# Routed expert blocks with deeper buffers: six row buffers instead of four, three weight buffers instead of two, and each block's rows issued one block earlier

## The chip, the cores and the metric

The kernel is one launch on 1 core of a Trainium2 chip. Its time is device microseconds (us), measured over whole executions; before the change the median of three is 2961.47 us (2958.9 to 2984.51). All durations below come from one further execution, taken with the hardware profiler.

## The reference

A layer stack on 8192 tokens (32 x 256) of width 128, in float32. Attention "a" works over the 256 positions of a sequence, attention "b" over the 32 rows at each position. After each of them comes the same expert layer:

```
x = x + attn_a(layernorm(x));  x = x + ffn(layernorm(x))
x = x + attn_b(layernorm(x));  x = x + ffn(layernorm(x))

_expert(h, g, u, d) = einsum('...i,hi->...h', silu(h @ g.T) * (h @ u.T), d)     # 128 -> 352 -> 128
scores, idx = top_k(softmax(x @ wr.T + rb), 2);  scores = scores / scores.sum()
ffn(x) = _expert(x, shared) + sum over the 2 chosen of 7 experts: score * _expert(x, rg[e], ru[e], rd[e])
```

So each token is computed by one shared expert and by two of seven routed ones.

## The kernel before, in words

There are two halves, A and B, one for each attention. In each half 16 passes of 512 tokens compute attention, the shared expert and the routing. A pass stores its result to DRAM (`x2` in half A, `out` in half B; the profile shows them as `x` and `out_x`) and scatters every token's normalised row twice, once for each chosen expert, into a DRAM buffer `sent`, sorted by expert. A row there has 132 floats: the 128 values, the weight of this expert for the token, and the token's number.

Then comes the **stage of the routed blocks**, the only part that the change touches. `sent` is read in NB = 38 blocks of 512 rows, each block all of one expert: 32 blocks' worth of rows plus up to 6 partly filled ones. A small table made on VectorE gives for block b the place of its rows, its expert (two of the four rows of `table`), and how many finished additions GpSimd must see before it adds the block's results. Each block goes through these steps:

- SyncE (queue SP) loads the rows `xs` (264 KB, line L778), the gate and up weights `w_gu` (704 KB, L784) and the down weights `w_dn` (192 KB, L788). Two table values, read into registers (L768, L769), give the addresses.
- TensorE (PE) turns the rows (`turn_x`, L1604), makes gate and up in three tiles each (`product`, three matmuls: L1528, L1529, L1530), the down product (`down`, L1630) and turns the result back (`turn_y`, L1638).
- ScalarE (ACT) and VectorE (DVE) copy, split and do the tanh and the products; ACT's `weigh` (L1043) multiplies the result by the expert's weight into `yo`, a ring of two.
- GpSimd (POOL) adds the block's 512 rows to DRAM in four indirect DMAs of 128 rows (`add_up`, L932), which add into `x2` or `out` at the token's number.

Every engine runs its own program of block bodies (`run_blocks`): PE's body b holds gate and up of block b, the turn of block b+1's rows, and the last two down tiles and the turn back of block b-1. So block b's rows are turned in body b-1, and its `weigh` is in ACT's body b+1. Body 0 stands alone, then LOOPED bodies, then a loop of LOOPED bodies an iteration, then the last.

What sets the order on SP is the program alone. For block b it waits until block b-4 has been turned, weighed and **added, with its additions landed in DRAM** (semaphore `added`, at L776), since the additions read the token numbers out of the row buffer; then it issues rows b. It waits until all gate and up products of block b-2 are done, issues `w_gu`; waits until the down products of b-2 are done, issues `w_dn`. The additions have two semaphores, for even and odd blocks.

POOL waits before block b for `yo` of b (`by_ready`) and for earlier additions. Two blocks that hold the same token must not be added at the same time; blocks of one expert never share a token. So the table asks, for a block whose expert differs from the block before, and for every block past the last expert's rows, that the additions of the block before have landed (here called a **guarded** block). For the others it asks only for block b-3's. The first blocks ask always (`early`). ACT's `weigh` of b waits until the additions of b-2 have landed, because it writes the same `yo` buffer.

## Time and profile before

| what | us |
|---|---|
| median of 3 runs | 2961.47 |
| profiled execution, its own time | 2964.5 |
| its span in the trace | 2962.7 |
| PE busy in the span | 2392.9 (81%) |
| DVE / ACT / POOL busy | 1664.2 / 1352.2 / 867.1 |
| routed blocks of half A, first block's addition to last's | 1172.98 to 1551.24 |
| routed blocks of half B, the same | 2573.56 to 2951.88 |

A profile row gives the engine, the line, what is written from what, the number of instructions and their time, and in brackets how long the engine was idle before and what ended it. A row named SPq is the issue of a DMA, not its transfer. PEclk is the clock that TensorE was granted, as a share of its full 2.4 GHz.

### The profile page before, as it was taken

What the parts mean: (1) busy time and instruction counts of PE and PEld (TensorE: products, weight loads), DVE (VectorE), ACT (ScalarE), POOL (GpSimd) and SP (SyncE); (2) the same over time, 40 slices, a digit from 0 to 9 for tenths busy, and PEclk for the clock granted to TensorE, in tenths of its full rate; (3) what the DMA queues carried; (4) which work ended last, traced back from release to release, by engine and by line L of the source; (5) the groups of instructions that cost most, each with busy time, mean ns of one, the idle gap of its engine ahead of it and who ended that gap; (6) DMA issues with size and microseconds to landing.
All of it is one profiled execution on the core that took longest, in us unless ns stands there. A gap on an engine that the chain in (4) does not pass through costs nothing.

```text
span 2962.7 us, 76346 instructions
## 1 busy us (share of the span) xinstructions
PE 2392.9 (81%) x26854; PEld 1597.4 (54%) x26854; DVE 1664.2 (56%) x6164; ACT 1352.2 (46%) x2861; POOL 867.1 (29%) x934
## 2 busy tenths in 40 slices
PE   7898988989898985888865768777778787588886
PEld 4565555656565653555543545555555555355553
DVE  4777777777777774444433554545454554444443
ACT  5787877778787871334332211222122211243333
POOL 3121111111111212665560112111211121255666
PEclk8898988888898997999985566655665665799998
DMA  5000000000000003666650000000000000466664
GB/s 194 31 22 17 20 16 21 16 17 16 17 16 20 20 16 113 144 139 141 138 105 12 21 17 24 21 21 17 23 22 21 17 22 19 121 141 141 147 138 93
DMA packets 129149, 168.52 MB, mean 57 GB/s; under 512 B 16240, under 2 KB 101104, under 8 KB 128800
## 3 DMA queue, kind: packets, MB, share of 16 engines
q1 hardware_dynamic: 59168, 118.08, 12.3%
q0 software_dynamic: 51968, 37.26, 8.8%
q10 hardware_dynamic: 17664, 8.39, 1.2%
q8 instruction: 235, 3.85, 0.6%
q14 instruction: 114, 0.93, 0.1%
HBM read 107.55 MB, written 56.12 MB: 55 GB/s over the span
## 4 chain that ended last, share of the span: by engine, by line
PE 60%; issue 12%; DVE 9%; DMA 8%; POOL 4%; ACT 4%; ACTq 1%; POOLq 1%; SPq 0%; DVEq 0%
PE bank_S L1445 5%; PE bank_E L1454 5%; PE bank_T L1454 4%; PE bank_E L1528 4%; PE bank_O L1468 4%; PE bank_O L1510 4%; PE bank_Y L1580 4%; PE bank_Y L1630 3%; DMA xs<-sent 3%; PE bank_E L1529 3%; PE bank_E L1530 3%; PE bank_E L1426 3%; PE bank_E L1417 2%; DMA out_x<-yo,xs 2%; DMA x<-yo,xs 2%
## 5 line engine op out<-in xcount | busy, mean ns | idle before, releaser
L973 ACT ACTIVATE z<-z,nm 128x256 f32<-128x256 f32 x1024 | 440.8, 500 | 115.5 <-DVE nm L1196 114.6
L1196 DVE CUSTOM_DVE_ANT_0 z<-bank_S,big 128x256 f32<-128x256 f32 x1024 | 380.4, 420 | 185.8 <-PE bank_S L1445 133.2
L868 POOL DMA_INDIRECT sent<-rows,slots x256 | 249.8, 976 | 249.6 <-DVE slots L1272 173.2
L932 POOL DMA_INDIRECT x<-yo,xs x152 | 237.1, 1560 | 183.0 <-ACT yo L1043 127.2
L932 POOL DMA_INDIRECT out_x<-yo,xs x152 | 236.1, 1553 | 182.5 <-ACT yo L1043 128.6
L1445 PE MATMUL bank_S<-kx,qx 32*128 32x256 f32 x1024 | 212.0, 369 | 75.8 <-issue 35.0
L1349 DVE SCALAR_TENSOR_TENSOR both<-both,bank_E 128x512 f32<-128x512 f32 (+1 forms) x228 | 156.5, 686 | 157.4 <-ACT both L1029 157.0
L853 POOL COPY seen<-seen 128x8 f32<-128x8 f32 x32 | 6.1, 191 | 761.3 <-DVE picked L1163 726.5
L1445 PEld LDWEIGHTS bank_S<-kx,qx 32*128 32x128 f32 x1024 | 129.2, 212 | 161.5 <-issue 92.7
L1029 ACT ACTIVATE both<-bank_E 128x512 f32<-128x512 f32 (+1 forms) x228 | 136.0, 597 | 170.0 <-PE bank_E L1530 166.1
L1528 PE MATMUL bank_E<-xbh,w_gu 128*128 128x512 f32 (+1 forms) x342 | 198.7, 581 | 2.9 <-DVE xbl L1342 2.9
L1510 PE MATMUL bank_O<-vx,probT 32*32 32x9 f32 x8192 | 118.4, 188 | 100.2 <-DVE probT L1230 85.1
L1510 PEld LDWEIGHTS bank_O<-vx,probT 32*32 32x32 f32 x8192 | 106.7, 131 | 155.9 <-issue 153.5
L1604 PE MATMUL bank_T<-cst,xs 128*128 128x128 f32 x304 | 57.9, 321 | 152.0 <-DMA xs<-sent 109.2
L1454 PE MATMUL bank_T<-cst,z 128*128 128x128 f32 x1024 | 178.4, 302 | 2.5 <-ACT probT L691 2.5
L1009 ACT ACTIVATE both<-bank_E 128x512 f32<-128x512 f32 (+1 forms) x96 | 57.3, 597 | 269.2 <-PE bank_E L1530 269.2
L1454 PE MATMUL bank_E<-cst,z 128*128 128x128 f32 x1024 | 178.3, 301 | 0.4
L691 ACT COPY probT<-bank_T 128x512 f32<-128x512 f32 x256 | 147.6, 577 | 40.9 <-PE bank_T L1454 38.1
L691 ACT COPY probT<-bank_E 128x512 f32<-128x512 f32 x256 | 150.2, 587 | 27.2 <-PE bank_E L1454 24.3
L1454 PEld LDWEIGHTS bank_T<-cst,z 128*128 128x128 f32 x1024 | 126.6, 152 | 48.4 <-issue 28.4
L1454 PEld LDWEIGHTS bank_E<-cst,z 128*128 128x128 f32 x1024 | 125.2, 152 | 49.1 <-issue 29.1
L1468 PE MATMUL bank_O<-probT,vx 128*32 128x256 f32 x2048 | 143.1, 398 | 5.3 <-ACT probT L691 5.2
(188 smaller groups left out, 5051.0 us busy)
## 6 DMA issues: line engine op xcount, KB each, us to landing
w_gu<-w_split SPq DMA_DIRECT2D x76, 704.0 KB, 4.3
xs<-sent SPq DMA_DIRECT2D x76, 264.0 KB, 2.7
w_dn<-w_split SPq DMA_DIRECT2D x76, 192.0 KB, 2.4
w_split<-w_gu SPq DMA_DIRECT2D x7, 704.0 KB, 3.1
both<-in_w_raw SPq DMA_DIRECT2D x8, 544.0 KB, 4.6
xin<-in_x SPq DMA_DIRECT2D x16, 256.0 KB, 2.9
sent<-rows,slots POOLq DMA_INDIRECT x256, 2.3
x<-xo ACTq DMA_DIRECT2D x16, 256.0 KB, 2.3
```

The source lines that it names most:

```text
L691: copy(probT[:, n % PT_RING, :], turn_bank(n)[:, :]).then_inc(emptied["T"], 1)
L868: pool.indirect_dma_start(out=sent, out_offset=bass.IndirectOffsetOnAxis(ap=slots[:, n:n + 1], axis=0), in_=rows[:, k, t, :], in_offset=No ...
L932: pool.indirect_dma_start(out=summed_in[kind], out_offset=bass.IndirectOffsetOnAxis(ap=xs_int[:, blk.four, t, COL_ID:COL_ID + 1], axis=0), ...
L973: last = act.activation(zt, zt, ACT.Exp, bias=nm[:, n % NM_RING, t:t + 1], scale=-1.0)
L1029: act.activation(th[0:m, n, :], in_blocks(2 * (3 * blk.k + n))[0:m, :], ACT.Tanh, scale=0.5).then_inc(bth_ready, 1)
L1196: last = dve.tensor_tensor_reduce(z[:, n % Z_RING, t * SEQ:(t + 1) * SEQ], bank[s][:, t * SEQ:(t + 1) * SEQ], bias_a[:, h, P - P * t:P - P ...
L1349: dve.scalar_tensor_tensor(out=a, in0=a, scalar=1.0, in1=in_blocks(q)[0:m, :], op0=ALU.add, op1=ALU.mult).then_inc(ba_ready, 1)
L1445: last = pe.matmul(bank[s][:, t * SEQ:(t + 1) * SEQ], qx[rows, p.two, g, lo:lo + P], kx[rows, p.two, g, b * SEQ:(b + 1) * SEQ], start=True ...
L1454: last = pe.transpose(turn_bank(n)[:, c:c + P], z[:, n % Z_RING, t * SEQ + k * P:t * SEQ + (k + 1) * P], ident)
L1468: last = pe.matmul(bank["O"][32 * j:32 * j + 32, 0:SEQ], vx[:, p.two, 2 * b + k, c:c + 32], probT[:, u % PT_RING, k * SEQ:(k + 1) * SEQ], ...
L1510: last = pe.matmul(bank["O"][r, h * VW:(h + 1) * VW], probT[r, h % 4, c:c + 32], vx[r, p.two, t, h * VW:(h + 1) * VW], start=True, stop=Tr ...
L1528: pe.matmul(dst, high_w, high_x, start=start, stop=False)
```

## The change

The three loads get deeper rings and a new order on SP. There are six row buffers (`X_RING`) instead of four and three weight buffers (`W_RING`) instead of two. SP issues the rows of block b+1 ahead of the weights of block b. The row load now waits for block b-6 to be turned, weighed and added, and the weight loads for the products of b-3. The loop holds six bodies, since its length must be a multiple of both rings. All engines index the new rings; their work per block is the same.

```diff
-LOOPED = 4
-X_RING = 4
+LOOPED = 6
+X_RING = 6
+W_RING = 3
...
-        self.two, self.four = k % 2, k % X_RING
+        self.two, self.six, self.w = k % 2, k % X_RING, k % W_RING
...
-    w_gu = sb("w_gu", [P, 2, GU], F32R)
-    w_dn = sb("w_dn", [P, 2, DN])
+    w_gu = sb("w_gu", [P, W_RING, GU], F32R)
+    w_dn = sb("w_dn", [P, W_RING, DN])
...
-                def body(blk, where):
+                def load_rows(blk):
+
                     at = sp.value_load(table[0:1, 0, bass.ds(blk.b, 1)], min_val=0, max_val=SPARE)
-                    e = sp.value_load(table[0:1, 1, bass.ds(blk.b, 1)], min_val=0, max_val=ROUTED - 1)
-
                     sp.wait_ge(bx_turned, blk.count(1, 1 - X_RING))
                     alone(sp)
                     sp.wait_ge(by_ready, blk.count(1, 1 - X_RING))
@@ -775,17 +775,24 @@
                     if blk.has_before(X_RING - 1):
                         sp.wait_ge(added[blk.two], blk.step(-X_RING).sums())
                     alone(sp)
-                    sp.dma_start(xs[:, blk.four, :, :], sent[bass.ds(at, BLOCK), :].rearrange("(p t) c -> p t c", t=TOK)
-                                 ).then_inc(rows_landed[blk.four], 16)
+                    sp.dma_start(xs[:, blk.six, :, :], sent[bass.ds(at, BLOCK), :].rearrange("(p t) c -> p t c", t=TOK)
+                                 ).then_inc(rows_landed[blk.six], 16)
+
+                def body(blk, where):
+                    if where == "first":
+                        load_rows(blk)
+                    if where != "last":
+                        load_rows(blk.step(1))
+                    e = sp.value_load(table[0:1, 1, bass.ds(blk.b, 1)], min_val=0, max_val=ROUTED - 1)
                     w = w_split[bass.ds(e, 1), :, :].rearrange("a p c -> (a p) c")
 
-                    sp.wait_ge(bup_done, blk.count(FT, -FT))
+                    sp.wait_ge(bup_done, blk.count(FT, (1 - W_RING) * FT))
                     alone(sp)
-                    sp.dma_start(w_gu[:, blk.two, :].bitcast(F32), w[:, 0:GU]).then_inc(gu_landed[blk.two], 16)
-
-                    sp.wait_ge(bdown_done, blk.count(FT, -FT))
+                    sp.dma_start(w_gu[:, blk.w, :].bitcast(F32), w[:, 0:GU]).then_inc(gu_landed[blk.w], 16)
+
+                    sp.wait_ge(bdown_done, blk.count(FT, (1 - W_RING) * FT))
                     alone(sp)
-                    sp.dma_start(w_dn[:, blk.two, :], w[:, GU:WROW]).then_inc(dn_landed[blk.two], 16)
+                    sp.dma_start(w_dn[:, blk.w, :], w[:, GU:WROW]).then_inc(dn_landed[blk.w], 16)
...
                 def turn_x(blk):
 
-                    pe.wait_ge(rows_landed[blk.four], 16 * blk.turn_of(X_RING))
+                    pe.wait_ge(rows_landed[blk.six], 16 * blk.turn_of(X_RING))
...
                 def gate(blk, n):
...
-                        pe.wait_ge(gu_landed[two], 16 * blk.turn_of(2))
+                        pe.wait_ge(gu_landed[blk.w], 16 * blk.turn_of(W_RING))
...
                 def down(blk, n):
...
-                        pe.wait_ge(dn_landed[blk.two], 16 * blk.turn_of(2))
+                        pe.wait_ge(dn_landed[blk.w], 16 * blk.turn_of(W_RING))
```

The order on SP at the first block of a half, before the change (TENSOR_LOAD reads a table value; a semaphore wait stands in brackets):

```order
L768 TENSOR_LOAD table [waits tails_stored]
L768 ISA x2
L769 TENSOR_LOAD table
L769 ISA x2
L778 ISA [waits bx_turned,by_ready]
L778 DMA xs<-sent 128x528
L784 ISA [waits bup_done]
L784 DMA w_gu<-w_split 128x1408
L788 ISA [waits bdown_done]
L788 DMA w_dn<-w_split 128x384
```

In the changed kernel the row load of the next block and one more table read come between the first rows and the first weights. The lines have moved: rows are L778, `w_gu` is L791, `w_dn` is L795.

The order on SP inside the loop, of the change (two blocks' worth; before it was table, table, rows, `w_gu`, `w_dn` of one and the same block):

```order
L770 TENSOR_LOAD table
L770 ISA x2
L771 REGISTER_ALU
L778 ISA [waits bx_turned,by_ready,added_1]
L778 DMA xs<-sent 128x528
L786 ISA
L786 TENSOR_LOAD table
L786 ISA x2
L789 REGISTER_ALU
L791 ISA [waits bup_done]
L791 DMA w_gu<-w_split 128x1408
L795 ISA [waits bdown_done]
```

Here the `xs` load is block b+1's and the two that follow are block b's, so the weights of b now stand behind a wait on the additions of block b-5. On POOL, ACT, DVE and PE every body holds the instructions that it held before, and a loop iteration holds six bodies instead of four.

## Rows read from the trace of the kernel before

**Rows 1.** The page: TensorE's granted clock in the 40 slices of the span.
```profile
PEclk8898988888898997999985566655665665799998
```

**Rows 2.** Busy time by stretch: length, each engine, granted clock, DMA share, GB/s.
```profile
1172.00:1558.00 386.00, 312.27 (x1157) 201.79 (x1156) 172.87 (x252) 146.22 (x329) 236.69 (x153) 0.91 0.60 134
1274.84:1283.49 8.65, 7.85 (x34) 5.09 (x33) 4.80 (x8) 4.05 (x11) 6.23 (x4) 1.00 0.67 160
1267.30:1271.40 4.10, 4.09 (x10) 2.61 (x11) 1.38 (x2) 1.19 (x2) 3.12 (x2) 0.58 0.71 179
```

**Rows 3.** Waits of all engines, 1180 to 1480 us: total, times, longest.
```profile
POOL x L932 <- ACT yo L1043: 78.4, 24, 5.4
PE bank_T L1604 <- DMA xs<-sent: 48.0, 29, 3.2
```

**Rows 4.** Timeline, POOL, additions of blocks 8 and 9: start, length, idle before.
```profile
1255.40 1.56 POOL L932 DMA_INDIRECT x<-yo,xs  x1 [4.43 <-ACT yo L1043]
...
1260.99 1.56 POOL L932 DMA_INDIRECT x<-yo,xs  x1 [0.30 <-issue]
1263.60 1.56 POOL L932 DMA_INDIRECT x<-yo,xs  x1 [1.05 <-ACT yo L1043]
```

**Rows 5.** Timeline around the row load of block 12.
```profile
1264.45 0.33 SPq L778 DMA_DIRECT2D xs<-sent  x1
1265.12 0.33 SPq L784 DMA_DIRECT2D w_gu<-w_split  x1
...
1267.31 0.97 PE L1604 MATMUL bank_T<-cst,xs 128*128 128x128 f32 x4 [2.77 <-DMA xs<-sent]
...
1277.60 0.66 PE L1604 MATMUL bank_T<-cst,xs 128*128 128x128 f32 x4 [0.80 <-DMA xs<-sent]
```

**Rows 6.** Timeline, PE: the first matmul of body 1 and of body 2.
```profile
1164.24 0.80 PE L1528 MATMUL bank_E<-xbh,w_gu 128*128 128x512 f32 x1
...
1171.85 0.79 PE L1528 MATMUL bank_E<-xbh,w_gu 128*128 128x512 f32 x1
```

**Rows 7.** Timeline, POOL: first addition of blocks 0, 1, 37 in half A, 0 in B.
```profile
1172.98 1.63 POOL L932 DMA_INDIRECT x<-yo,xs  x1 [34.70 <-ACT yo L1043]
...
1182.76 1.56 POOL L932 DMA_INDIRECT x<-yo,xs  x1 [2.53 <-DMA x<-yo,xs]
...
1551.24 1.56 POOL L932 DMA_INDIRECT x<-yo,xs  x1 [2.52 <-DMA x<-yo,xs]
...
2573.56 1.62 POOL L932 DMA_INDIRECT out_x<-yo,xs  x1 [33.11 <-ACT yo L1043]
```

**Rows 8.** Chain of waits, 2900 to 2963 us (POOLq: POOL's sequencer); blocks 32, 36, 37.
```profile
2903.59 1.20 POOL out_x L932
2904.83 0.29 POOLq L923
...
2947.68 3.33 DMA out_x<-yo,xs
...
2951.88 1.55 POOL out_x L932
```

**Rows 9.** Timeline, DMA issues on SP at the start of half A's blocks.
```profile
1151.48 0.36 SPq L778 DMA_DIRECT2D xs<-sent  x1
1152.09 0.35 SPq L784 DMA_DIRECT2D w_gu<-w_split  x1
1152.69 0.33 SPq L788 DMA_DIRECT2D w_dn<-w_split  x1
...
1154.51 0.33 SPq L778 DMA_DIRECT2D xs<-sent  x1
```

**Rows 10.** The view of line L784, 1180 to 1560 us: issue of `w_gu` to landing.
```profile
DMA to landing us min/median/max: 3.9/4.4/6.5
```

**Rows 11.** The view of line L778, the same stretch: issue of `xs` to landing.
```profile
DMA to landing us min/median/max: 2.6/2.8/3.1
```

**Rows 12.** The view of line L932, the whole span: issue of an addition to landing.
```profile
DMA to landing us min/median/max: 3.2/3.4/6.1
```

More of the change, by code:

```diff
@@ L621, in program @@
     rows_landed = [sem(f"rows_landed_{k}") for k in range(X_RING)]
-    gu_landed, dn_landed = ([sem(f"{n}_landed_{k}") for k in range(2)] for n in ("gu", "dn"))
+    gu_landed, dn_landed = ([sem(f"{n}_landed_{k}") for k in range(W_RING)] for n in ("gu", "dn"))
     bx_turned, bxh_ready, bxl_ready = (sem(n) for n in ("bx_turned", "bxh_ready", "bxl_ready"))
@@ L933, in add_up @@
                             out=summed_in[kind], out_offset=bass.IndirectOffsetOnAxis(
-                                ap=xs_int[:, blk.four, t, COL_ID:COL_ID + 1], axis=0),
+                                ap=xs_int[:, blk.six, t, COL_ID:COL_ID + 1], axis=0),
                             in_=yo[:, blk.two, t, :], in_offset=None, compute_op=ALU.add).then_inc(added[blk.two], 16)
@@ L1043, in weigh @@
                         last = act.activation(yo[:, blk.two, t, :], bank["O"][:, t * P:(t + 1) * P], ACT.Copy,
-                                              scale=xs[:, blk.four, t, COL_W:COL_W + 1])
+                                              scale=xs[:, blk.six, t, COL_W:COL_W + 1])
                     last.then_inc(by_ready, 1)
@@ L1599, in turn_x @@
                 def turn_x(blk):
-                    pe.wait_ge(rows_landed[blk.four], 16 * blk.turn_of(X_RING))
+                    pe.wait_ge(rows_landed[blk.six], 16 * blk.turn_of(X_RING))
                     pe.wait_ge(bxl_ready, blk.count(1, 0))
                     for t in range(TOK):
-                        last = pe.transpose(bank["T"][:, t * P:(t + 1) * P], xs[:, blk.four, t, 0:D], ident)
+                        last = pe.transpose(bank["T"][:, t * P:(t + 1) * P], xs[:, blk.six, t, 0:D], ident)
                     last.then_inc(bx_turned, 1)
@@ L1610, in gate @@
                         pe.wait_ge(bxl_ready, blk.count(1, 1))
-                        pe.wait_ge(gu_landed[two], 16 * blk.turn_of(2))
+                        pe.wait_ge(gu_landed[blk.w], 16 * blk.turn_of(W_RING))
                     pe.wait_ge(ba_ready, blk.count(FT, n - 1))
-                    hi, lo = gate_up(w_gu[:, two, :], n, 0)
+                    hi, lo = gate_up(w_gu[:, blk.w, :], n, 0)
                     product(in_blocks(2 * (3 * blk.k + n))[0:m, :], hi, lo, xbh[:, two, :], xbl[:, two, :]
@@ L1619, in up @@
                     pe.wait_ge(bh_ready, blk.count(FT, n - 1))
-                    hi, lo = gate_up(w_gu[:, two, :], n, 1)
+                    hi, lo = gate_up(w_gu[:, blk.w, :], n, 1)
                     product(in_blocks(2 * (3 * blk.k + n) + 1)[0:m, :], hi, lo, xbh[:, two, :], xbl[:, two, :]
@@ L1626, in down @@
                     if n == 0:
-                        pe.wait_ge(dn_landed[blk.two], 16 * blk.turn_of(2))
+                        pe.wait_ge(dn_landed[blk.w], 16 * blk.turn_of(W_RING))
                         pe.wait_ge(bsummed, blk.count(1, -1))
                     pe.wait_ge(bh_ready, blk.count(FT, n + 1))
-                    pe.matmul(down_bank(blk)[:, :], w_dn[0:m, blk.two, n * P:(n + 1) * P], hid[0:m, n, :],
+                    pe.matmul(down_bank(blk)[:, :], w_dn[0:m, blk.w, n * P:(n + 1) * P], hid[0:m, n, :],
                               start=(n == 0), stop=(n == FT - 1)).then_inc(bdown_done, 1)
```

## The prediction

> **What bounds the kernel now.** Only the two stages of routed blocks are touched: 378.3 us from the first addition of block 0 to that of block 37 in half A (1172.98 to 1551.24) and 378.3 in half B (2573.56 to 2951.88) [rows 7, 8]. That is 37 steps of 10.22 us on average.
>
> I read the stretch view first. Over half A's stage PE is busy 312 of 386 us, POOL 237, DVE 173, ACT 146, the DMA engines 0.60 of the time [rows 2]. Nothing is full, so the stage is held by a loop of waits. The waits view names it: PE waits for the rows `xs` before it turns them, 48 us in 300, and POOL for ACT's `yo`, 78 us in 300, which is the echo of PE's lateness further down [rows 3].
>
> The timeline shows why the rows are late. The additions of block 8 start at 1255.40, the fourth of them at 1260.99 [rows 4]; it lands some 3.4 us later [rows 12]; and SP issues the rows of block 12, which go into the same buffer, at 1264.45, 9.05 us behind block 8's first addition [rows 5]. They take 2.8 us [rows 11] and PE has by then stood for 2.77 us, in the next body for 0.80 [rows 5]. After the long stand the clock is at 0.58 for some 4 us, that is mostly its lower level of 1.2 GHz; in the next body it is 1.00, 2.4 GHz [rows 2]. So the ring of four row buffers is the loop: addition of b-4, landing, rows of b, turn in body b-1, results in body b+1, addition of b.
>
> What would the loop allow at full clock? 9.05 to the issue, 2.8 to the turn, then 5.8 for the rest of body b-1 (1277.60 to 1283.4, [rows 2, 5]), a whole body of 7.6 [rows 6], and some 8.9 in body b+1 to `yo` and the addition (an estimate: the weighing stands at the end of that body, a POOL start comes some 0.8 behind it). 34 us for four blocks are 8.5 a block; the rest of the 10.2 are the stands of the other chains and the slow clock.
>
> **The change, part by part.**
>
> *Six row buffers.* The same 34 us are spread over six blocks, 5.7 a block, less than any engine's own work. The stands on rows go. What is late next is the engine with the most work per block:
>
> - PE: body 1, which had its rows early, lasts 1171.85 - 1164.24 = 7.61 us [rows 6]; the 8.65 of body 12 less its 0.8 to 1.0 of stand gives 7.7 to 7.85 [rows 2, 5].
> - POOL: four additions of 1.56 with 0.30 between them are 3 x 1.86 + 1.56 = 7.15 us [rows 4], plus the gap to the next block. Its price isn't seen, since POOL nearly always waits for `yo` at that place. Above it is bounded by 1.05, the gap when `yo` was hardly late [rows 4], below by 0.30, the gap inside a block. I take 0.30: the chain of waits shows POOL's sequencer reading the next block's table value (L923) at 2904.83, 1.24 us behind block 32's first addition and long before the other three run [rows 8]. So it runs ahead of the engine, and with `yo` early the next block's additions can queue up behind. An unguarded block then takes 7.45 us.
> - A guarded block can't be queued ahead. From block 0 to 1 it is 1182.76 - 1172.98 = 9.78 us [rows 7], made of three additions of 1.86, a landing of 3.33 (2947.68 to 2951.01) and 0.87 to the next start [rows 8]. Its landing runs beside more traffic than now: the DMA share goes from 0.60 to 0.60 x 386 / 310 = 0.75. I add 0.2 us to it: 10.0.
>
> In number: two guarded at the start, six changes of expert, and those past the last expert's rows. The last additions, block 37's among them [rows 7], stand 2.5 to 2.8 us on DMA, three in half A and two in half B. So 11 in A and 10 in B, and 26 and 27 unguarded ones.
>
> Sum for A: 26 x 7.45 + 11 x 10.0 = 193.7 + 110 = 303.7, from 378.3: 74.6 saved. For B: 27 x 7.45 + 100 = 301.2: 77.1 saved. PE needs 37 x 7.65 = 283, so POOL sets the pace. Already the first two guarded blocks put it 2 x (9.8 - 7.65) = 4 us behind PE, and in an unguarded block it gains only 0.2 back. How far it may fall behind is limited by the two `yo` buffers: `yo` of b is written from 9.0 us behind the first addition of b-2, ready at 10.2, and startable at 11.0, while POOL comes to it at 14.9. So 3.9 us stay in hand and PE does the waiting.
>
> *Three weight buffers, and the new order.* Weights were not what PE waited for; all its DMA waits before the turn are on rows [rows 3]. But now `w_gu` of b stands behind the row load of b+1 and so behind the additions of b-5. That chain: 9.05 to the rows' issue, some 1.3 (the issue distance of 0.67 [rows 5] and a table read of 0.6, below), 4.4 to landing [rows 10], then body b and most of body b+1, 16.5: 31 us over five blocks, 6.3 a block; with the longest landing of 6.5, 6.7. Under 7.45, so no cost.
>
> *Start of a half.* Between block 0's rows and its `w_gu` come now another row load and a table read. SP took 0.6 from issue to issue without table reads and 1.82 with two [rows 9], so a read is 0.6, and `w_gu` of block 0 goes out 1.2 us later. PE began body 0 at about 1156.6 (one body of 7.6 before body 1 [rows 6]), and a landing of 4.4 had the weights there at 1156.5; now it is 1157.7 or, behind the second rows, later. I take 1.0 us of delay a half, 2 in all; bounds 0.6 and 2.
>
> *Loop of six bodies.* Fewer iterations, the same work. I price it at nothing: no body's start showed a wait there that the next one didn't.
>
> Total: 74.6 + 77.1 - 2 = 149.7 us. The profiled execution took 2964.5, 3 above the median of 2961.47, so 2964.5 - 149.7 = **2815 us**, a gain of 5%.
>
> **The rivals.**
>
> *POOL doesn't run ahead across blocks.* For it: the table read and two semaphore waits stand between two blocks, and no row shows a gap under 1.05 there [rows 4]. Then 53 unguarded blocks take 0.7 us more: +37, 2852 us.
>
> *Additions land later.* Three sets of weights may now be in flight beside them. The longest landing was 6.1 against a median of 3.4 [rows 12]. If all 21 guarded blocks paid it, 2.7 each, less the 0.2 that I took: +53, 2868 us. Against it: the stage already had the DMA engines at 0.60 and the median stayed at 3.4. The Trainium skill's page "DMA: Bandwidth & Descriptors" (Queues, rings and completion order) states that a completion increment lands only after every earlier write of that DMA engine, across its queues. By that rule the additions' increments would wait for weight writes in front of them, which is this rival; no row shows which write an increment waited for.
>
> *PE stays in the way.* When PE waits for POOL, its clock may fall, as after the 2.77 us stand [rows 2]. The granted clock in attention, where PE is also nearly full, is only 0.8 to 0.9 [rows 1]. At 0.85 a body takes 7.65 / 0.85 = 9.0, and 37 of them 333 instead of 303: +60, 2875 us.
>
> *The change doesn't do what it says:* some other wait of similar length stands behind the one on rows, such as the weights through DMA crowding, and each step stays near 10. Then 2955 to 2965. The chain of 31 us over five blocks would have to be 50, which no landing here explains.
>
> *Slower.* The mechanism is the clock alone: if short waits of PE on POOL in every body keep it mostly at the lower level, a body takes 7.65 divided by the granted share, and it decides from 7.65 / 10.22 = 0.75 downward. At 0.70 a step is 10.9, 37 are 404: 26 more a half, 3016 us. For it: half B's attention shows 0.5 to 0.6 in a dozen slices [rows 1]. Against it: with 0.80 us of stand in body 12 the clock stayed 1.00 [rows 2, 5], and PE would be busier than now.
>
> **How the numbers follow.** The forecast has 0.44, POOL's gap 0.22, late landing 0.12, PE's clock 0.12, no effect 0.04, slower 0.03, and 0.03 for something better than forecast (fewer guarded blocks, or none felt), about 2790. From 2800 to 2878 hold the first four with their bounds. A change of this kernel can be told from none at about 1%, 30 us; all cases but the last two on the bad side are faster by more: 0.93, within 1% 0.04, slower 0.03.
>
> **What would show it.** Right: PE's wait on `xs` is nearly gone; POOL's busy share in the stage is above 0.75; the first additions of an unguarded block start 0.3 us behind the last one's end, with the releaser no longer ACT; ACT or PE waits on the landing of additions; the stage is about 303 us. Wrong: gaps of 1 us at every block (the first rival), guarded steps well over 10 (the second), PE still waiting on `xs` or now on `w_gu`, or a granted clock under 0.9 with PE never waiting for POOL (the third). What would break the forecast most is an order between POOL's queue and its engine that the trace of before can't show.

## The result: 4.2% faster, 30 us short of the forecast

| | before | after |
|---|---|---|
| median of runs on one chip, us | 2966.13 (2958.9 to 2984.51, 4 runs) | 2845.52 (2840.89 to 2849.38, 4 runs) |
| ratio, 95% interval | | 0.9584 [0.9534, 0.9633] |
| profiled execution, its span | 2964.5, 2962.7 | 2840.89, 2839.1 |
| blocks of half A, first addition to last block's | 378.3 | 316.3 |
| blocks of half B, the same | 378.3 | 314.0 |
| first row load of a half to its first addition, A / B | 21.5 / 20.6 | 23.0 / 24.8 |

The forecast was 2815 with a range of 2800 to 2878. Against the profiled execution of before, the stages give 61.9 and 64.4 us back (forecast 74.6 and 77.1), and the starts of the halves take 1.5 and 4.2 (forecast 1.0 each). The rest of the difference of 123.6 is 3.0 us of attention passes: half A's took 8.1 us less and half B's 5.1 more in this execution.

### The profile after

First additions of block 0 and block 37 in each half, of the timeline of POOL; the answer to [rows 7]:

```profile
1166.43 1.63 POOL L939 DMA_INDIRECT x<-yo,xs  x1 [35.56 <-ACT yo L1050]
...
1482.75 1.56 POOL L939 DMA_INDIRECT x<-yo,xs  x1 [2.56 <-DMA x<-yo,xs]
...
2514.33 1.62 POOL L939 DMA_INDIRECT out_x<-yo,xs  x1 [37.43 <-ACT yo L1050]
...
2828.28 1.55 POOL L939 DMA_INDIRECT out_x<-yo,xs  x1 [2.78 <-DMA out_x<-yo,xs]
```

Busy time by stretch (length; PE, PEld, DVE, ACT, POOL; granted clock, DMA share, GB/s): half A's stage, and a run of unguarded blocks in it. The answer to [rows 2]:

```profile
1166.00:1488.00 322.00, 282.96 (x1156) 183.71 (x1154) 165.28 (x251) 140.17 (x328) 235.52 (x151) 0.97 0.71 155
1222.00:1273.00 51.00, 46.89 (x192) 30.24 (x191) 28.30 (x44) 23.19 (x56) 42.77 (x28) 1.00 0.81 178
```

POOL has the same 236 us of work as before, now in 322 us, and in the run of unguarded blocks it is busy 42.77 of 51: 84%, which is all that four instructions of 1.56 with gaps of 0.30 can be (1.56 / 1.86). PE's clock rose from 0.91 to 0.97.

The waits in the same stretch (total, times, longest); the answer to [rows 3]:

```profile
ACT yo L1050 <- DMA x<-yo,xs: 99.8, 33, 7.3
POOL x L939 <- DMA x<-yo,xs: 43.3, 11, 6.0
POOL x L939 <- ACT yo L1050: 35.6, 1, 35.6
...
PE bank_E L1535 <- DMA w_gu<-w_split: 13.1, 14, 2.3
```

PE's wait on `xs` is gone from the list. POOL waits for `yo` a single time, before block 0; else it stands only on the landing of its own earlier additions, 11 times, once for each guarded block. ACT's `weigh` stands on the same landings: it is now early and waits for a free `yo` buffer. The direction of the pipeline has turned round: before, POOL waited for the rest; now the rest waits for POOL. A small new wait of PE on `w_gu` is there too; it doesn't reach POOL, which in half A waits for `yo` nowhere else.

The timeline of POOL from the first addition of block 5. Blocks 6 to 13 follow; 6 and 14 are guarded, with a new expert. The answer to [rows 4]:

```profile
1208.31 1.56 POOL L939 DMA_INDIRECT x<-yo,xs  x1 [0.30 <-issue]
...
1213.91 1.56 POOL L939 DMA_INDIRECT x<-yo,xs  x1 [0.30 <-issue]
1221.28 1.56 POOL L939 DMA_INDIRECT x<-yo,xs  x1 [5.81 <-DMA x<-yo,xs]
...
1228.73 1.56 POOL L939 DMA_INDIRECT x<-yo,xs  x1 [0.31 <-issue]
...
1251.10 1.56 POOL L939 DMA_INDIRECT x<-yo,xs  x1 [0.30 <-issue]
...
1266.01 1.56 POOL L939 DMA_INDIRECT x<-yo,xs  x1 [0.30 <-issue]
...
1286.45 1.56 POOL L939 DMA_INDIRECT x<-yo,xs  x1 [5.80 <-DMA x<-yo,xs]
```

From block 6 to block 7 it takes 1228.73 - 1221.28 = 7.45 us, with 0.31 before block 7: the gap between two blocks is as short as the gap inside one. From block 5 to block 6 it takes 1221.28 - 1208.31 = 12.97, of which 5.81 are spent waiting for a landing.

The row loads of blocks 12, 13, 16 and 18 in the timeline of SP. Each waits for the landing of the additions of the block six earlier (6, 7, 10, 12); the answer to [rows 5]:

```profile
1230.37 0.33 SPq L778 DMA_DIRECT2D xs<-sent  x1
...
1238.14 0.33 SPq L778 DMA_DIRECT2D xs<-sent  x1
...
1263.40 0.33 SPq L778 DMA_DIRECT2D xs<-sent  x1
...
1278.76 0.33 SPq L778 DMA_DIRECT2D xs<-sent  x1
```

These rows are a gauge for how late additions land. Behind block 6's first addition the row load comes 1230.37 - 1221.28 = 9.09 us later, as before the change. Behind block 7's it is 9.4, behind block 10's 12.3 (1263.40 - 1251.10), behind block 12's 12.75 (1278.76 - 1266.01). I call this distance the **landing gauge**; 9.1 is its undisturbed value. For a guarded block it is back at 9.1 (block 6), and it grows again over the next four or five blocks. In the chain of waits one late landing stands by itself, before block 21:

```profile
1336.79 5.63 DMA x<-yo,xs
```

Before the change that piece was 3.33 [rows 8]. The issues of the page (count, KB, us to landing; 5.4 answers to the 4.4 of [rows 10]):

```profile
w_gu<-w_split SPq DMA_DIRECT2D x76, 704.0 KB, 5.4
xs<-sent SPq DMA_DIRECT2D x76, 264.0 KB, 2.8
w_dn<-w_split SPq DMA_DIRECT2D x76, 192.0 KB, 5.3
```

And the start of half A's blocks on SP (x2: the rows of blocks 0 and 1), the answer to [rows 9]: `w_gu` of block 0 goes out 2.45 us behind the first rows, before it was 0.61.

```profile
1143.40 1.64 SPq L778 DMA_DIRECT2D xs<-sent  x2
1145.85 0.33 SPq L791 DMA_DIRECT2D w_gu<-w_split  x1
```

### The profile page after: what moved, and what is told of

The parts are those of the page before. It is cut to its first block, busy times and chain, and to the rows that moved or that the text cites. A ratio compares the mean times of both kernels' runs of the same rounds, so it can differ in the third digit from the quotient of the medians.

```text
span 2839.1 us, 76148 instructions
## 1 busy us (share of the span) xinstructions
PE 2338.6 (82%) x26854; PEld 1574.7 (55%) x26854; DVE 1649.9 (58%) x6164; ACT 1342.0 (47%) x2861; POOL 867.0 (31%) x934
## 4 chain that ended last, share of the span: by engine, by line
PE 56%; issue 15%; POOL 10%; DVE 9%; DMA 4%; ACT 3%; POOLq 1%; ACTq 1%; DVEq 0%; SPq 0%
PE bank_S L1452 6%; POOL out_x L939 5%; POOL x L939 5%; PE bank_E L1461 5%; PE bank_T L1461 5%; PE bank_O L1517 4%; PE bank_O L1475 4%; PE bank_Y L1587 4%; PE bank_E L1535 3%; PE bank_E L1433 3%; PE bank_E L1424 3%; PE bank_E L1536 2%; DMA out_x<-yo,xs 2%; PE bank_E L1537 2%; PE bank_S L1499 2%
## 5 line engine op out<-in xcount | busy, mean ns | idle before, releaser
L939 POOL DMA_INDIRECT x<-yo,xs x152 | 237.1, 1560 | 121.9 <-DMA x<-yo,xs 43.3
L1535 PE MATMUL bank_E<-xbh,w_gu 128*128 128x512 f32 (+1 forms) x342 | 178.4, 522 | 38.7 <-DMA w_gu<-w_split 25.5
L1050 ACT ACTIVATE yo<-bank_O,xs 128x128 f32<-128x128 f32 x304 | 86.7, 368 | 190.2 <-DMA x<-yo,xs 99.8
L842 POOL COPY h1F<-h 128x512 f32<-128x512 f32 x32 | 19.6, 612 | 418.6 <-DVE h L1222 225.3
```

The source lines that it names most:

```text
L939: pool.indirect_dma_start(out=summed_in[kind], out_offset=bass.IndirectOffsetOnAxis(ap=xs_int[:, blk.six, t, COL_ID:COL_ID + 1], axis=0), ...
L1535: pe.matmul(dst, high_w, high_x, start=start, stop=False)
```

## The experiments

A step is the time from one block's first addition to the next one's. The first eight runs were made on two other chips, where the attention passes take longer (the kernel before: 3237.16 and 3246.24 us) while the stages of the blocks have the lengths known from here; so ratios and stage lengths are compared, and totals named in the expectations are some 275 us low for them. The last four were made on one more chip, where the kernel before took 2962.76; e9 and e10 are one run each, so their ratios have no interval.

| run | median, us | ratio to before, same chip | stage A / B, us |
|---|---|---|---|
| e1, six row buffers alone | 3113.63 | 0.9614 [0.9579, 0.9648] | 319.4 / 321.3 |
| e2, third weight buffer alone | 3243.33 | 1.0021 [0.9997, 1.0045] | 381.5 / 375.9 |
| e3, new order alone | 3446.62 | 1.0641 [1.0601, 1.0681] | 482.0 / 476.5 |
| e4, weight loads of 16 columns | 3071.94 | 0.9488 [0.9439, 0.9536] | 302.2 / 298.9 |
| e5, every block guarded | 3210.56 | 0.9894 [0.9865, 0.9922] | 364.8 / 365.4 |
| e6, three additions | 3042.01 | 0.9374 [0.9348, 0.9401] | 282.9 / 282.6 |
| e7, weights of block 0 first | 3114.17 | 0.9592 [0.9569, 0.9614] | 318.1 / 312.9 |
| e8, e7 and two guards less | 3104.63 | 0.9560 [0.9536, 0.9584] | 316.1 / 307.8 |
| r9, the change again | 2845.59 | 0.9617 [0.9589, 0.9646] | 317.8 / 312.1 |
| r10, e8 again | 2834.19 | 0.9584 [0.9556, 0.9612] | 315.8 / 308.9 |
| e9, e5 with later weights | 2953.34, one run | 0.997 (2953.34 / 2962.76) | 367.2 / 368.6 |
| e10, half of the weights | 2827.77, one run | 0.954 (2827.77 / 2962.76) | 301.8 / 301.4 |

### Which part brings the gain

**Six row buffers alone**, in the kernel before:

```diff
-LOOPED = 4
-X_RING = 4
+LOOPED = 6
+X_RING = 6
```

> The kernel before with only the row ring changed, four to six buffers (and the loop of six bodies that goes with it); two weight buffers and the old order on SP stay. Theory A (the rows' ring was the whole loop, and POOL is the bound after it): PE's wait on xs goes, unguarded steps of POOL are 7.46 us, each half about 315 us from the first addition to the last, as in the changed kernel, and the start of a half stays at 21 us from the first row load to the first addition; time about 2838 us, 5 below the changed kernel. Rival B (the third weight buffer was needed too): PE waits for w_gu in every body, steps of 8.2 us and more, time 2865 us or above.

Measured: 0.9614, stages 319.4 and 321.3. Steps of 7.4 to 7.5 are there as in the full change, but in the longest stretches of one expert some are 8.2 to 9.4. The waits of half A's stage (1309 to 1629) show what is late in them:

```profile
PEld bank_T L1604 <- DMA xs<-sent: 39.3, 35, 2.0
POOL x L932 <- DMA x<-yo,xs: 36.3, 13, 4.9
PE bank_T L1604 <- DMA xs<-sent: 24.1, 34, 1.6
```

The rows are still a little late, in every body (PE 34 times, 24.1 us together; before it was 29 times and 48.0 us in 300 us, [rows 3]). So the ring of six carries nearly all of the gain, and the rest of the change takes 3 us off half A's stage and 7 off half B's (316.3 and 314.0). That small part was seen as lengths of single executions, not timed against one another; the half's later start takes some 2 us of it back, and as whole ratios e1 (0.9614) and the change (0.9584, and 0.9617 in r9) can't be told apart.

**The third weight buffer alone**, with the old order and four row buffers:

```diff
-LOOPED = 6
-X_RING = 6
+LOOPED = 12
+X_RING = 4
...
-                    if where == "first":
-                        load_rows(blk)
-                    if where != "last":
-                        load_rows(blk.step(1))
+                    load_rows(blk)
```

> The changed kernel with four row buffers again and the old order on SP: only the third weight buffer is left (loop of twelve bodies). Theory A: PE still stands for the rows of every block, a half stays at 378 us, time within 5 us of the kernel before. Rival B (weights were half of it): a half at 350 us, time about 2905.

Measured: 1.0021 [0.9997, 1.0045], stages 381.5 and 375.9: nothing. PE stands on the rows as before (1306 to 1688):

```profile
POOL x L936 <- ACT yo L1047: 129.8, 22, 35.2
...
PE bank_T L1608 <- DMA xs<-sent: 58.6, 19, 4.0
```

**The new order alone**, with rings of four and two:

```diff
-LOOPED = 6
-X_RING = 6
-W_RING = 3
+LOOPED = 4
+X_RING = 4
+W_RING = 2
```

> The changed kernel with four row buffers and two weight buffers: only the order is left, rows of block b+1 issued ahead of the weights of block b. Theory A: now the weights of b stand behind the additions of b-3; by the chain 9.05 + 1.3 + 4.4 + 16.5 = 31 us over three blocks a step is 10.4 us, PE waits for w_gu instead of xs, and a half is 385 us or a little more, time 2975 to 3000. Rival C (issuing rows earlier is worth something by itself): a half under 370 us, time under 2950.

Measured: 1.0641, stages 482.0 and 476.5, far above what I expected. Steps alternate between 7.6 and, mostly, 18 to 20. The waits (1350 to 1700) and then the chain of waits (start, length, piece):

```profile
PE bank_E L1535 <- DMA w_gu<-w_split: 124.3, 15, 9.7
```

```profile
1393.04 3.35 DMA x<-yo,xs
...
1397.97 4.94 DMA w_gu<-w_split
...
1403.03 0.79 PE bank_E L1535
1403.82 0.43 PE bank_E L1536
...
1408.90 0.24 PE bank_E L1535
...
1410.30 0.45 PE bank_O L1645 x4
...
1412.80 1.22 POOL x L939
...
1418.39 3.37 DMA x<-yo,xs
...
1423.32 5.07 DMA w_gu<-w_split
```

One turn of the loop, from `w_gu` to `w_gu`, is 1423.32 - 1397.97 = 25.35 us, and it moves on by **two** blocks. My count of such a chain, in the prediction as well, let the weights of block b hold up only block b's own results, at the end of body b+1. But PE runs its bodies in order, and body b also holds the last down tiles and the turn back of block b-1 (the `bank_O` piece at 1410.30). When PE stands at the head of body b for weights, it holds back the `yo` of block b-1, whose additions come 1412.80 - 1402.91 = 9.9 us behind the landing. So additions of m release the rows of m+4 and, behind them in SP's queue, the weights of m+3; those release the `yo` of m+2: some 9.1 + 1.3 + 5 + 9.9 = 25.3 us over two blocks, 12.7 a block. After each long stand the next matmuls take 0.43 where later ones take 0.24, which is the lower clock; the stage's mean is 0.83.

With six row buffers the same chain runs over four blocks: 9.1 + 1.4 + 5.2 + about 9 = 24.7, 6.2 a block. This is hidden under POOL's 7.45, and nearly not: where the landing gauge stands at 12.8 it is 28.4, 7.1 a block. That fits PE's 14 short waits on `w_gu` above. The single longer step in the packed blocks, that of block 29 (7.8 in the list below, 9.7 in r9), has another origin: POOL pauses inside block 28, between its first and second addition, for 0.57 to 2.55 us in both halves of the traces of the change, e7, e8, r9 and r10. The profile shows nothing that it waits for there; the cause stays open.

### What makes a guarded step long

The steps of the changed kernel (first trace, half A, blocks 1 to 37; a guarded block marked by a star):

```
9.8* 9.7* 7.5 7.5 7.5 13.0* 7.5 7.5 7.5 7.5 7.5 7.5 7.5 13.0* 7.5 7.5 7.5 7.5 7.5 7.5 12.2* 9.9*
7.5 7.5 7.5 12.2* 7.5 7.5 7.8 7.5 13.2* 7.5 7.5 7.5 9.8* 9.7* 9.7*
```

Eleven guarded steps, as counted, but 122.1 us instead of 110. The long ones come at the end of a **packed run**, two or more unguarded blocks one behind the other. But block 35 ends one too, of the same length as the one before block 6, and its step is 9.8; so does block 36 in half B (9.8). By then no weights are left to load: the last `w_gu` went out 15.6 us ahead of the fourth addition that block 35 waits for, and 25.4 us ahead of block 36's in half B. The first question was whether the weights do it.

**Weight loads of 16 columns** from block 4 on (the rest of each buffer keeps an earlier block's weights):

```diff
+                    cut = GU if where in ("first", "early") else 16
-                    sp.dma_start(w_gu[:, blk.w, :].bitcast(F32), w[:, 0:GU])
+                    sp.dma_start(w_gu[:, blk.w, 0:cut].bitcast(F32), w[:, 0:cut])
...
+                    cut = min(cut, DN)
-                    sp.dma_start(w_dn[:, blk.w, :], w[:, GU:WROW])
+                    sp.dma_start(w_dn[:, blk.w, 0:cut], w[:, GU:GU + cut])
```

> The changed kernel, but from block 4 on each weight load moves only 16 of the columns (64 B a partition instead of 5632 and 1536), so the outputs use old weights; rows and additions are as they were. In the changed kernel a guarded step that follows a run of packed additions takes 11.2 to 13.8 us (ten in all, 127.6 us), the others 9.6 to 9.9. Theory D (the additions fall behind because the weight transfers share the DMA engines with them): all guarded steps are 9.7 to 9.9, each half loses about 15 us, time about 2812. Rival E (four indirect additions in 7.46 us are themselves more than the DMA queue drains): guarded steps stay at 12 to 13 us, time unchanged at about 2842.

Measured: every guarded step is 9.7 to 10.1, the landing gauge 9.0 to 9.3 everywhere, the stages 302.2 and 298.9, against my forecast of 303.7 and 301.2. The busy times of a packed run show the same POOL and a DMA share of 0.56:

```profile
1361.00:1412.00 51.00, 51.00 (x214) 34.36 (x213) 30.89 (x47) 27.08 (x61) 42.77 (x28) 1.00 0.56 70
```

The packed additions are the same ones, one every 1.86 us. So additions alone don't come late; the weight transfers beside them make them late.

**Every block guarded**, with all the weights:

```diff
-                        add_up(blk.step(-1), where == "early")
+                        add_up(blk.step(-1), True)
...
-                        add_up(blk, False)
+                        add_up(blk, True)
```

> The changed kernel with every block guarded: POOL waits at each block until the additions of the block before have landed. No run of packed additions is left, the weight and row traffic per block stays. Theory D1 (the late landing is a backlog that builds over a run of packed additions): every step is 9.7 to 9.9 us, a half 37 x 9.8 = 362 us, time about 2935. Rival F (a landing is late whenever weight transfers run beside it, run or no run): steps of 11 to 13 us, a half over 410 us, time over 3030.

Measured: steps of 9.6 to 9.9, with 8 of 74 between 10.2 and 11.4, the gauge at 9.0 to 9.3 (once 10.5). With whole weights nearly all landings are in time. But three are late with no packed run at all: the steps of block 33 in both halves (11.4 and 11.3) and of block 4 in half B (11.1). And one objection stood. In this kernel `w_gu` always goes out 4.9 us ahead of a block's fourth addition (in the rows of POOL and SP), which is about its time to landing, so that it is out of the way when that one starts.

**The same, with SP waiting for the next block's rows to land** before it issues `w_gu`:

```diff
+                    if where not in ("first", "early", "last"):
+                        sp.wait_ge(rows_landed[blk.step(1).six], 16 * blk.step(1).turn_of(X_RING))
+                        alone(sp)
                     sp.dma_start(w_gu[:, blk.w, :].bitcast(F32), w[:, 0:GU])
```

> Every block guarded, as in the run of that name, whose steps were 9.7 to 9.9; in addition SP waits, from block 4 on, until the rows of the next block have landed before it issues w_gu. With every block guarded w_gu went out 4.9 us ahead of the fourth addition; now it goes out 2.0 to 2.4 ahead, so that its 704 KB are on the engines while that addition lands. Theory D1 (additions are late only behind the backlog that a packed run builds up): steps stay 9.7 to 10.2, stages 365 to 375 us. Theory D2 (an addition lands late whenever weights are in flight beside it, and the run of all guarded blocks escaped by its phase): steps of 11 to 13, stages 410 to 470 us.

Measured: 65 of 74 steps between 9.6 and 10.1, the stages 367.2 and 368.6, the gauge at 9.0 to 9.5 (three times 10.4 to 10.8). The two longest steps, 12.5 and 12.7, are again those of block 33. One block in the timelines of POOL and of SP:

```profile
1228.79 1.56 POOL L942 DMA_INDIRECT x<-yo,xs  x1 [0.30 <-issue]
1232.86 1.56 POOL L942 DMA_INDIRECT x<-yo,xs  x1 [2.51 <-DMA x<-yo,xs]
```

```profile
1225.38 0.33 SPq L794 DMA_DIRECT2D w_gu<-w_split  x1
```

The shift came out smaller than meant, `w_gu` 3.4 us ahead of the fourth addition and not 2.0 to 2.4; PE starts the next body, on these weights, at 1229.94, when the addition that began at 1228.79 is still on its way. So the weights overlap that landing in part only, and it comes no later. Block 33 is where the overlap is fuller: at the end of a half no row load holds SP back, and the weights of blocks 36 and 37 go out one behind the other, at 1480.92 and 1482.81, the second 1.6 us ahead of block 32's fourth addition. The landing then takes POOL 5.34 us of waiting:

```profile
1484.39 1.56 POOL L942 DMA_INDIRECT x<-yo,xs  x1 [0.30 <-issue]
1491.29 1.56 POOL L942 DMA_INDIRECT x<-yo,xs  x1 [5.34 <-DMA x<-yo,xs]
```

```profile
1482.81 0.33 SPq L794 DMA_DIRECT2D w_gu<-w_split  x1
```

So a landing can be late without a packed run, and this run doesn't exclude D2: in nearly all of its blocks the weights were out of the way in time.

**Half of the weight columns** in the changed kernel, from block 4 on:

```diff
+                    half = 1 if where in ("first", "early") else 2
-                    sp.dma_start(w_gu[:, blk.w, :].bitcast(F32), w[:, 0:GU])
+                    sp.dma_start(w_gu[:, blk.w, 0:GU // half].bitcast(F32), w[:, 0:GU // half])
...
-                    sp.dma_start(w_dn[:, blk.w, :], w[:, GU:WROW])
+                    sp.dma_start(w_dn[:, blk.w, 0:DN // half], w[:, GU:GU + DN // half])
```

> The changed kernel, but from block 4 on the weight loads bring half of the columns (352 and 96 KB instead of 704 and 192; the other half keeps what an earlier block left there, so the results of those blocks are not the reference's). With 16 columns the guarded steps were 9.7 to 10.1, with all of them 11.2 to 13.8. D1, a backlog that only builds near full load: the DMA share in a packed run falls from 0.81 to about 0.63, and the guarded steps are 9.7 to 10.6, stages 302 to 307 us. D2, each addition waits for the weight bytes in flight beside it: half of the lateness stays, guarded steps 10.5 to 11.8, stages 307 to 311 us.

Measured: all guarded steps 9.7 to 10.0, the gauge 9.0 to 9.3, stages 301.8 and 301.4. (The routing of half B depends on half A's results, so here some other blocks of half B are guarded.) The packed run is as packed as ever, with `w_gu` 2.3 to 2.7 us ahead of every fourth addition in it. Its busy times:

```profile
1222.00:1273.00 51.00, 51.00 (x213) 34.21 (x212) 31.28 (x48) 27.16 (x62) 42.62 (x28) 1.00 0.70 125
```

At a DMA share of 0.70 nothing is late; at 0.81 the last landing comes 3 us late. Half of the weights takes away all of the lateness, so it isn't in proportion to the weight bytes, as D2 was priced. But the run doesn't show a backlog (D1) either, since it changes the timing too: half a `w_gu` lands 4.0 us behind its issue (median), a whole one 5.4. Issued some 2.6 us ahead of the fourth addition, the half is there 1.4 us behind that addition's start, well before it lands.

**Backlog or timing.** The trace of the change says more. Busy times inside its packed run, just ahead of block 12's first addition, then the share of the DMA engines by queue from 1267.00 to 1268.50 (q1 carries SyncE's loads, q0 GpSimd's additions), and the fourth addition of block 12 beside the nearest `w_gu`:

```profile
1263.75:1264.25 0.50, 0.50 (x5) 0.40 (x4) 0.00 (x0) 0.50 (x4) 0.20 (x2) 1.00 0.00 0
```

```profile
q1 hardware_dynamic: 94, 0.52, 90.4%
q0 software_dynamic: 21, 0.01, 5.6%
```

```profile
1271.61 1.56 POOL L939 DMA_INDIRECT x<-yo,xs  x1 [0.30 <-issue]
```

```profile
1272.19 0.34 SPq L791 DMA_DIRECT2D w_gu<-w_split  x1
```

The DMA engines stand empty for half a microsecond, deep in the run that begins with block 6 and with the gauge already above 12. So no backlog of bytes waits at them from block to block. The second view covers the time at which block 11's fourth addition (started at 1264.15) would land undisturbed: the engines are busy with loads, and the additions get almost nothing. Call the **lead** the time by which `w_gu` goes out ahead of the nearest fourth addition. In the two traces of the change (blocks 3 to 31) a lead of 4.5 us and more goes with a gauge of 9.0 to 9.2 in 21 of 22 cases (once 9.7), a lead of 2.6 to 2.7 with 9.2 to 11.6, and a lead under 0.5 with 11.4 to 13.0. From block 7 to block 13 of half A, in the first trace, the lead falls: 2.6, 2.3, 0.6, 0.1, -0.6, -0.6, -1.1.

That points at D2 in another form: an addition is late when whole weights are in flight as it lands, and one late landing makes the next. SP issues the next `w_gu` behind a row load that waits for the landing, so a late landing shortens the next lead. It would also explain why the gauge stops at about 13: `w_gu` is by then issued behind the fourth addition. The late landings outside packed runs (block 33 in e5 and e9) and the timely ones at the end of a half (blocks 35 and 36 above) fit this and not a backlog. Not every row does: step 4 of half B in e5 is 11.1 with a lead of 4.8, and three gauges in e9 are 10.4 to 10.8 at the same lead as the rest. The reading was not tested by a run of its own; a packed run in which `w_gu` keeps a lead of 5 us would do it.

### What sets the pace

**The fourth addition left out** (so a quarter of the rows is not added), with the counts that belong to it:

```diff
-                    for t in range(TOK):
+                    for t in range(TOK - 1):
                         pool.indirect_dma_start(
```

> The changed kernel with the fourth addition of every block left out, so a quarter of the routed results is missing from the outputs. POOL's work falls from 7.46 to 5.6 us a block. Theory A (POOL sets the pace): PE sets it now, unguarded steps are 7.7 to 8.0 us, ACT waits little for landings, a half is about 290 us, time about 2792. Rival G (PE, the weights or the yo buffers set it already): a half falls by less than 10 us, time 2820 or more.

Measured: 0.9374, stages 282.9 and 282.6. The busy times of half A's stage:

```profile
1312.00:1595.00 283.00, 276.48 (x1156) 186.47 (x1154) 165.98 (x251) 145.89 (x328) 173.06 (x111) 0.99 0.73 167
```

PE is busy 276.5 of 283 us. So POOL set the pace of the changed kernel, as forecast, and PE's own 37 x 7.65 = 283 us lie right under it: 31 to 33 us a half below the change. Guarded steps of 10 to 12 stand beside steps of 5.6 in which POOL catches up, so that here they cost next to nothing: a late landing is paid only because POOL has no slack.

### The start of a half, and a better version

**Weights of block 0 ahead of the rows of block 1**:

```diff
                     if where == "first":
                         load_rows(blk)
-                    if where != "last":
+                    elif where != "last":
                         load_rows(blk.step(1))
...
                     sp.dma_start(w_dn[:, blk.w, :], w[:, GU:WROW]).then_inc(dn_landed[blk.w], 16)
+                    if where == "first":
+                        load_rows(blk.step(1))
```

> The changed kernel with one difference at the start of a half: block 0's rows, then block 0's weights, then block 1's rows. In the changed kernel the first row load to the first addition took 23.0 and 24.8 us in the two halves, against 21.5 and 20.6 before. Theory H (all of it is w_gu of block 0 issued later): 21 us in both halves again, time about 5 us under the changed kernel, 2837. Rival: the traffic of the further loads delays it anyway, under 2 us gained.

**The same, and in half B the blocks 1 and 2 ask the table** instead of always waiting for the additions of the block before:

```diff
-                        add_up(blk.step(-1), where == "early")
+                        add_up(blk.step(-1), where == "early" and (kind == "A" or blk.k == 1))
```

> e7 and one thing more: in half B the blocks 1 and 2 ask the table whether they must wait for the block before, as all later blocks do, instead of always waiting. Theory A: POOL sets the pace, so the two guarded steps of 9.7 us become 7.5 to 7.7 and half B is 4 us shorter, time 4 us under e7, about 2833. Rival: the longer packed run gives a later landing at the next guarded block and takes 1 to 2 us of it back.

Measured: the start of a half, from first rows to first addition, is 23.0, 24.8, 25.1 and 23.0 in the two traces of the change, mean 24.0; with the weights first it is 22.3, 22.8, 22.6, 22.5 and (in r10) 22.1 and 21.6, mean 22.3. Before it was 21.5 and 20.6. The order of the two loads explains some 1.6 of the 2.9 us a half. I had expected all of it, 21 us again; the rival, under 2 us gained, came true, and the rest stays open. Half B's first two steps fall from 9.7 and 9.6 to 7.5 and 7.5, and its stage is 5.1 us shorter than in e7, 3.2 shorter in r10 than in r9. The rival, a later landing at the next guarded block, doesn't show clearly: step 6 of half B is 12.6 against 12.8 in e7, and 13.4 in r10 against 12.0 in r9. POOL's timeline in r10 from its first addition in half B; the gap before the fifth one, block 1's first, is 0.30 now:

```profile
2507.02 1.62 POOL L941 DMA_INDIRECT out_x<-yo,xs  x1 [34.45 <-ACT yo L1052]
...
2514.56 1.55 POOL L941 DMA_INDIRECT out_x<-yo,xs  x1 [0.30 <-issue]
```

**The change, and this version, on one chip:**

> The changed kernel once more, on the chip of the next three runs. It left a ratio of 0.958 to the kernel before; on a chip with longer attention passes I expect 0.961 to 0.965, stages of 316 and 314 us, and guarded steps after a packed run of 11.2 to 13.8 us as in its first trace. If those lengths are random from execution to execution, they come at other blocks now; if they follow the program, at the same ten blocks (A: 6, 14, 21, 26, 31, 35; B: 6, 13, 22, 26, 32, 36) with the same sizes within 1 us.

> The changed kernel with two edits: at the start of a half the weights of block 0 are issued ahead of the rows of block 1, and in half B the blocks 1 and 2 ask the table instead of always waiting for the additions of the block before. From its first trace: stage B 308 us against 314, the start of each half 1 to 2 us shorter. That should make it 6 to 10 us faster than the changed kernel on the same chip, a ratio 0.002 to 0.003 lower. If the earlier difference of 10 us came from noise in the attention passes, the two come out the same within 3 us.

Measured: 2845.59 (2844.04 to 2853.7) against 2834.19 (2828.57 to 2843.39), five and six runs: 11.4 us faster than the change, 0.4%. The two ratios to before are 0.0033 apart, and their intervals overlap, since both carry the scatter of before; the ranges of the runs themselves don't. It is the fastest of the complete kernels here. The change's long guarded steps came at the same ten blocks as in its first trace; my list in the expectation has two wrong entries, 35 and 36, the two that end a packed run with no weights left to load. Seven of the ten agree within about 0.5 us; three differ by 0.5 to 1.5, so a single size holds for one execution only.

## Why the prediction was right, and what was mis-sized

- **The bound of before** (the ring of four row buffers): right. Six buffers alone give a ratio of 0.9614.
- **POOL paces the unguarded blocks at 7.45**: right, 7.46 in half A and 7.43 in half B. The disputed gap between blocks is 0.30, the lower bound that I took from the sequencer's early table read [rows 8]. The rival "POOL doesn't run ahead" is out.
- **Number of guarded blocks**, 11 and 10: right. The nine that don't follow a packed run, and the two at the end of a half that do, took 9.6 to 9.9, under the 10.0 that I gave them.
- **The step that failed: "I add 0.2 us to it: 10.0".** The other ten guarded steps took 11.2 to 13.8, 127.6 us together, for which I had 100. In the sum, the guarded blocks took 122.1 + 113.0 = 235.1 instead of 210: 25 us of the miss. I had reckoned the traffic as the mean share of a whole stage (0.75; it was 0.71). A guarded block asks at the end of a packed run, where the share is 0.81 and `w_gu` goes out as late as 1.2 us behind the fourth addition that it asks for. e4 and e10 show that the weight loads are what makes that landing late; that it is their timing and not a backlog is the reading that fits the rows, untested. The median landing of 3.4 [rows 12] told nothing of that: before the change `w_gu` went out 3.9 us or more ahead of every fourth addition.
- **The rival "additions land later"** named the cause and gave 2.7 us to all 21; it came true for the ten, with 2.8 over 10.0 on average. The Trainium skill's page "DMA: Bandwidth & Descriptors" (Queues, rings and completion order), named there for this rival, says that a completion lands only after all earlier writes of that DMA engine. The trace agrees as far as it goes: the additions are late where whole weights are in flight as they land. No row shows which write an increment waited for, and in the view by queue above the additions' own transfers hardly run beside the loads, so these runs don't test the rule in itself.
- **Weights cost nothing**: held, with less in hand than I wrote. My chain of 31 us over five blocks should have been 24.7 over four, since weights of b hold back the results of b-1. It gives 6.2 a block and not 6.3, the same for this ring, but the same mistake made my expectation for the order alone wrong by some 95 us a stage. PE's 13.1 us of waits on `w_gu` are in POOL's shadow.
- **Start of a half, 1.0 us each**: 1.5 and 4.2, mean 2.9 with the second trace, above the upper bound of 2. I had one row load and one table read between the first rows and `w_gu`, 1.2 us. It is one row load and two reads: the read of the expert, which stood ahead of the first rows before, has moved behind them too (the section on the change says one more read as well), and `w_gu` goes out 2.45 - 0.61 = 1.84 us later. That the weights then share the engines with the second rows I mentioned and didn't price. Moving them ahead gets 1.6 back.
- **Clock**: right. 0.97 in the stage, 1.00 in a packed run; the two clock rivals are out.

The sum of the errors: 25 us in the guarded steps and 4 in the starts, with 3 given back by the attention passes, make the 26 us between forecast and profiled execution; the median of the runs lies 5 above that execution. The unguarded steps were forecast within 0.5 us a half.

## What to carry to other kernels

Deepening a ring moves the bound to the next engine, and what that engine waits for then meets a load that the old trace never had: price such a wait by what is in flight at the moment when it is asked (here whole weights, at the end of a packed run), not by the mean of the stage. A deeper ring also moves loads against the waits that they used to miss. When loads for different blocks stand in one queue, follow the chain through the consumer's program order: a wait at the head of a body also holds back the previous block's results that are finished in it, which shortens the loop by a block. And issue what a first block needs ahead of what the second one needs.

## What was not expected of the hardware

- Indirect additions beside weight loads: while SyncE's loads took 90.4% of the DMA engines' time, GpSimd's additions got 5.6% (1267.00 to 1268.50 in the change), and the landing that was due then came some 3 us late. With whole weights and a short lead the gauge goes to 11.4 to 13.0; with a lead of 4.5 us and more it is 9.0 to 9.2, and with half weights, at a DMA share of 0.70 (125 GB/s) against 0.81 (178 GB/s), 9.0 to 9.3 everywhere. The row loads still take 2.8 us, and `w_gu` 5.4 instead of 4.4.
- GpSimd's sequencer passes a table read and two semaphore waits while the engine works on queued additions: 0.30 us between blocks, the same as inside a block.
- Chips differ: the kernel before took 3237 us on one and 2963 on another. The difference lies in the attention passes (half A's first row load came at 1287.0 us in e1, at 1144.5 in r9); the block stages have the same lengths within 1% (half A in e7 and r10, where the two kernels are the same: 318.1 and 315.8).
